# Attention and feed-forward kernel: queries made up to three slots ahead, projection first in a slot, transpose back behind the division

## The reference

```python
def _layernorm(x): return (x - mean(x)) / sqrt(var(x) + eps)      # over the last axis
x = x + attention(_layernorm(x), ctx, ctx, mask)                  # 16 heads of 16, scores: exp(log_C) * tanh(q.k * scale / 4)
x = x + ffn(_layernorm(x))
def ffn(x):
    gf = sigmoid-net of x.mean(axis=1)                            # 3 layers, per batch
    out = x
    for _ in range(3):
        tf = sigmoid-net of out                                   # 4 layers, per token
        coupling = 0.1 + adaptive_range * (0.7*gf + 0.3*tf - 0.5) * 2.0
        out = out + coupling * twist(out)                         # [p_r, -p_i, -o_r, o_i]
    return out
```

## Time and profile before

| | |
|---|---|
| median of 3 runs | 1152.38 us (1148.89 to 1153.36) |
| profiled execution | 1158.11 us, span 1156.2 us |
| mean granted TensorE clock | 0.964 |
| TensorE matmul busy | 998.3 us (86%) |
| ScalarE busy | 928.4 us (80%) |
| VectorE busy | 793.2 us (69%) |
| GpSimd busy | 584.0 us (51%) |
| 16 DMA engines, mean | 13.0% |

### The profile page before, as it was taken

How to read it: one execution, slowest core, us unless ns; L and a number is a source line. 1 busy time by engine, 2 the same in 40 slices (tenths; PEclk the granted TensorE clock), 3 DMA queues, 4 the chain that set the end, 5 groups by cost and what they waited for, 6 DMA issues and landing times.

```text
span 1156.2 us, 21972 instructions
## 1 busy us (share of the span) xinstructions
PE 998.3 (86%) x7260; PEld 536.9 (46%) x7260; DVE 793.2 (69%) x1738; ACT 928.4 (80%) x1153; POOL 584.0 (51%) x1117
## 2 busy tenths in 40 slices
PE   6889988899888998889888898888988889886894
PEld 4555435544455434554355543555435544453431
DVE  4876677757687485874858749577577757676285
ACT  5999679887798777987779877898679887794576
POOL 4577107871188602895048830688207871175303
PEclk8999999999999998999999999999999999997897
DMA  4110002210022100211002200122001220010002
GB/s 129 45 42 19 1 2 68 65 50 1 1 69 69 46 1 2 89 48 46 1 24 69 69 23 2 45 70 69 0 1 47 69 68 1 1 42 28 19 1 74
DMA packets 67281, 43.85 MB, mean 38 GB/s; under 512 B 42081, under 2 KB 50785, under 8 KB 67169
## 3 DMA queue, kind: packets, MB, share of 16 engines
q1 hardware_dynamic: 67168, 42.45, 13.0%
HBM read 25.51 MB, written 16.78 MB: 37 GB/s over the span
## 4 chain that ended last, share of the span: by engine, by line
PE 41%; DVE 21%; issue 14%; ACT 12%; POOL 10%; SPq 1%; DVEq 0%; DMA 0%; POOLq 0%; ACTq 0%
PE ps L1098 7%; PE ps L1143 7%; PE ps L1130 7%; PE ps L1156 5%; ACT probs L835 5%; PE ps L1067 4%; DVE move_u L727 4%; PE ps L1083 3%; ACT probs L841 3%; DVE coup L693 2%; DVE f_t L731 2%; PE ps L1186 2%; DVE move_u L706 2%; DVE move_v L708 2%; PE ps L1165 2%
## 5 line engine op out<-in xcount | busy, mean ns | idle before, releaser
L835 ACT ACTIVATE probs<-ps,u_scale 120x2048 f32<-120x2048 f32 x128 | 253.4, 1980 | 41.5 <-PE ps L1067 40.7
L841 ACT ACTIVATE probs<-probs,exp_bias,clip 120x2048 f32<-120x2048 f32 x128 | 269.5, 2106 | 0.1
L1156 PE MATMUL ps<-h,w 128*128 128x512 f32 x384 | 184.2, 605 | 14.0 <-ACT h L867 13.2
L1067 PE MATMUL ps<-q_t,k_t 32*120 32x256 f32 x2048 | 154.0, 416 | 32.0 <-ACT probs L835 31.2
L447 POOL TENSOR_TENSOR c<-tok_c 128x16 f32<-128x16 f32 x8 | 1.8, 222 | 330.7 <-issue 330.7
L637 DVE STREAM_TRANSPOSE o_t<-ps 128x512 f32<-128x512 f32 x128 | 91.2, 712 | 99.7 <-PE ps L1083 99.6
L1098 PE MATMUL ps<-wo_t,of_t 128*128 128x256 f32 x512 | 149.1, 417 | 8.5 <-DVE of_t L657 8.5
L1083 PE MATMUL ps<-probs,va 120*32 120x256 f32 x2048 | 140.2, 392 | 4.7 <-ACT probs L841 4.7
L1067 PEld LDWEIGHTS ps<-q_t,k_t 32*120 32x120 f32 x2048 | 96.1, 184 | 61.7 <-issue 56.3
L1098 PEld LDWEIGHTS ps<-wo_t,of_t 128*128 128x128 f32 x512 | 94.1, 204 | 44.6 <-issue 26.4
L498 POOL TENSOR_TENSOR f_hl<-f_t,f_hl 128x512 f16<-128x512 f32 x64 | 73.7, 1162 | 79.9 <-DVE f_hl L684 79.9
(11 more groups left out here) (129 smaller groups left out, 1849.6 us busy)
## 6 DMA issues: line engine op xcount, KB each, us to landing
xy<-in_x_dram SPq DMA_DIRECT2D x64, 256.0 KB, 2.9
out_dram<-xy SPq DMA_DIRECT2D x64, 256.0 KB, 2.0
cbuf<-in_ctx_dram SPq DMA_DIRECT2D x64, 120.0 KB, 2.7
tok_c<-coup SPq DMA_DIRECT2D x256, 0.5 KB, 2.0
move_v<-in_L_xattn_W_out_dram SPq DMA_DIRECT2D x1, 256.0 KB, 5.3
move_u<-in_L_ffn_cn_w_dram SPq DMA_DIRECT2D x1, 256.0 KB, 5.6
w<-in_L_ffn_cn_w_dram SPq DMA_DIRECT2D x1, 128.0 KB, 5.5
g<-in_L_ffn_gc_w_dram SPq DMA_DIRECT2D x1, 128.0 KB, 4.0
```

The costliest lines, as they stand in the source:

```text
L835: eng.activation(probs[:, b % 2, n * HALF:(n + 1) * HALF, :].rearrange("k h q -> k (h q)"), banks(SCORE_BANK, 4)[0:KEYS, :], ACT.Tanh, sca ...
L841: eng.activation(p, p, ACT.Exp, scale=clip[0:KEYS, 0:1], bias=exp_bias[:, b:b + 1]).then_inc(s_exp, 1)
L1067: last = eng.matmul(banks(SCORE_BANK + r)[0:KEYS, odd * S:(odd + 1) * S], k_t[rows, b % 2, odd, n, :], q_t[rows, b % 2, n, :], start=True, ...
L1156: last = eng.matmul(banks(bank), w2[:, k, :], h1[:, p % 2, k, :], start=(k == 0), stop=(k == EK - 1))
```

## The change

- q_hat and its statistics get four buffers (QR). Three queries a group instead of one are made in the feed-forward stage (early+2 to early+4, two before high half 2, one before high half 3); the slots at 0, 1 and 4 make none, the slots at 2 and 3 make that of i+3, the others that of i+2. Slots before 11 go on making i+2.
- GpSimd's query_hat is split into query_scale and query_hat, norm_2 into norm_2_scale and norm_2, factors into twisted_part and x_part, and they are put in another order within a slot.
- VectorE runs residual(i-2) and stats_2(i-2) first in a slot, and attn_features(i-1) directly behind divide(i-1), one slot earlier than before. The high halves move from the slots at 3 and 5 to those at 2 and 4.
- TensorE runs project(i-2,0) and project(i-2,1) directly behind scores(i,0). keys(i+1) stays behind scores(i,1), weighted_values(i-1,1) follows it.
- SyncE loads before it stores, and the load of i+4 that fell into the slot at 0 is issued in the feed-forward stage.

```diff
+    QR = 4
...
-        mv1 = sb("mv1", [P, 2, TT, 2])
+        mv1 = sb("mv1", [P, QR, TT, 2])
...
-        q_hat = sb("q_hat", [P, 2, TT, E])
+        q_hat = sb("q_hat", [P, QR, TT, E])
...
-        HIGH_AT = (3, 5)
+        HIGH_AT = (2, 4)
...
+        def ahead_in_slot(i):
+
+            if i < GROUP + LAG:
+                return i + 2 if i >= 0 else None
+            at = (i - LAG) % GROUP
+            return None if at in (0, 1, 4) else i + 3 if at < 4 else i + 2
+
+        def ahead_in_ffn(g):
+
+            early = g * GROUP + GROUP + LAG
+            return [b for b in range(early + 2, early + 5) if b < NB]
...
                 if kind != "attention":
+                    for b in ahead_in_ffn(i)[2:]:
+                        load(b)
                     coupling_rows(i)
...
-                for b in late[:1]:
-                    store(b)
-                late = late[1:]
...
-                elif 0 <= i + 4 < NB and i >= -1:
+                elif 0 <= i + 4 < NB and i >= -1 and not after_ffn(i):
                     load(i + 4)
+                for b in late[:1]:
+                    store(b)
+                late = late[1:]
...
                 if kind == "ffn":
-                    early = i * GROUP + GROUP + LAG
-                    if early + 2 < NB:
-                        query_hat(early + 2)
-                    for chunk in (2, 3):
-                        for k in range(EK):
-                            low_half(i, chunk, k)
+                    ahead = ahead_in_ffn(i)
+                    for b in ahead[:2]:
+                        query_scale(b)
+                        query_hat(b)
+                    for k in range(EK):
+                        low_half(i, 2, k)
+                    for b in ahead[2:]:
+                        query_scale(b)
+                        query_hat(b)
+                    for k in range(EK):
+                        low_half(i, 3, k)
...
                 if 0 <= i - LAG < NB:
+                    norm_2_scale(i - LAG)
+                    if after_ffn(i):
+                        norm_2(i - LAG)
+                        coefficients(groups_before(i) - 1)
+                for b in late[:1]:
+                    twisted_part(b)
+                if 0 <= i - LAG < NB and not after_ffn(i):
                     norm_2(i - LAG)
-                if i == early:
-                    coefficients((i - LAG) // GROUP - 1)
+                if new is not None and 2 <= new < NB:
+                    query_scale(new)
                 for b in late[:1]:
-                    factors(b)
+                    x_part(b)
                 late = late[1:]
                 if 0 <= i + 1 < NB:
                     values(i + 1)
...
+                if new is not None and 2 <= new < NB:
+                    query_hat(new)
...
-                    new, nxt, here, old = i + 2, i + 1, i - 1, i - 2
+                    new, nxt, here, old = ahead_in_slot(i), i + 1, i - 1, i - 2
...
+                    if 0 <= old < NB:
+                        residual(old)
+                        stats_2(old)
                     if 0 <= here < NB:
                         attn_out(here, 0)
-                    if 0 <= old < NB:
-                        attn_features(old)
                     if 0 <= nxt < NB:
                         queries_out(nxt)
                         keys_out(nxt)
-                    if 2 <= new < NB and i != early:
+                    if new is not None and 2 <= new < NB:
                         stats(new)
                     if 0 <= here < NB:
                         attn_out(here, 1)
-                    if 0 <= old < NB:
-                        residual(old)
-                    if 0 <= here < NB:
                         divide(here)
-                    if 0 <= old < NB:
-                        stats_2(old)
+                        attn_features(here)
                     for b in late[:1]:
                         combine(b)
...
-                    early = i * GROUP + GROUP + LAG
-                    if early + 2 < NB:
-                        stats(early + 2)
+                    ahead = ahead_in_ffn(i)
+                    for b in ahead[:2]:
+                        stats(b)
                     high_half(i, 2)
+                    for b in ahead[2:]:
+                        stats(b)
                     high_half(i, 3)
...
                     if 0 <= i < NB and i != early:
                         scores(i, 0)
+                    if 0 <= old < NB:
+                        project(old, 0)
+                        project(old, 1)
                     if 0 <= here < NB:
                         weighted_values(here, 0)
...
                     if 0 <= nxt < NB:
                         keys(nxt)
-                    if 0 <= old < NB:
-                        project(old, 0)
                     if 0 <= here < NB:
                         weighted_values(here, 1)
-                    if 0 <= old < NB:
-                        project(old, 1)
                     if 0 <= i - LAG < NB:
                         norm_to_features(i - LAG)
```

More of the change, by code:

```diff
@@ L422, in norm_2 @@
                 eng.tensor_tensor(rstd2[:, at, :], var2[:, b % 2, :], minus_half[:], ALU.pow).then_inc(s_rstd2, 1)
+            def norm_2(b):
+                at = b % XR
                 eng.wait_ge(s_neg2, b + 1)
@@ L499, in low_half @@
                    .then_inc(s_flo, 1)
-            early, late = None, []
+            late = []
             for kind, i in slots():
                 if kind == "ffn":
-                    early = i * GROUP + GROUP + LAG
-                    if early + 2 < NB:
-                        query_hat(early + 2)
-                    for chunk in (2, 3):
-                        for k in range(EK):
-                            low_half(i, chunk, k)
+                    ahead = ahead_in_ffn(i)
[9 more added lines that the diff above has]
+                        low_half(i, 3, k)
                     late = list(range(i * GROUP, (i + 1) * GROUP))
                     continue
-                if 0 <= i - LAG < NB:
+                new = ahead_in_slot(i)
+                if i == -2:
+                    for b in range(2):
+                        query_scale(b)
+                        query_hat(b)
+                if 0 <= i - LAG < NB:
+                    norm_2_scale(i - LAG)
[5 more added lines that the diff above has]
+                if 0 <= i - LAG < NB and not after_ffn(i):
                     norm_2(i - LAG)
-                if i == early:
-                    coefficients((i - LAG) // GROUP - 1)
+                if new is not None and 2 <= new < NB:
+                    query_scale(new)
                 for b in late[:1]:
-                    factors(b)
+                    x_part(b)
                 late = late[1:]
@@ L757, in end_combine @@
                    .then_inc(s_res, 1)
-            late, early = [], None
+            late = []
             for kind, i in slots():
```

47 lines of the change are left out of this document (23 added, 24 removed).

## The result

| | before | after |
|---|---|---|
| median | 1152.79 us (4 runs, 1148.89 to 1153.36) | 1168.71 us (4 runs, 1167.17 to 1170.21) |
| profiled execution | 1158.11 us, span 1156.2 us | 1167.66 us, span 1165.9 us |
| mean granted TensorE clock | 0.964 | 0.986 |

The changed kernel is slower: the ratio is 1.0145, 95% interval 1.0118 to 1.0173. The forecast was 1220 us with a range of 1178 to 1260, so the side was right and the size was far off.

A forecast was written before the change was run, and what follows sets the result against it. ScalarE's 8.39 us of work was taken to bound a slot, with 35 us lost to late q_hat. From the 1152.4 us median, +32 without the clock and +37 for it (+69) gave 1220 us, range 1178 to 1260.

The forecast's parts named there:

- The ring: Attention slots: residual(i-2), all of VectorE's slot, project(i-1) on TensorE, residual(i-1) form a closed chain of 10.0 us against 8.39.
- Its length: The closed chain's step times in an attention slot, summed: 10.0 us with new stats, 9.5 us without.
- a step that needs the result just made is its duration + 0.10: Rule for dependent VectorE steps, start to start: 0.10 us added to the duration, as reciprocal 0.35, next 0.45 later.
- the sum without the clock: Whole kernel before any clock loss: slots 2 to 10 +14.4, groups +23, feed-forward starts -2, last group +3.5, drain -7; +32.
- The clock: TensorE idling before projections lowers its clock: 1.0 us per slot with stats, 0.25 without, +37 us.
- If it falls in the middle of the projection, about 1.4 us of that runs at half speed: TensorE's projection after 1.9 us idling: low clock adds 1.4 us a slot, bounds 0 and 1.9, taken as 1.0 with stats.
- the first rival: TensorE's idle pieces come out shorter or spread, so the slot chain costs without clock loss: 1184 us, chance 0.2.
- The second rival: Low TensorE clock in nearly every attention slot, 54 x 1.4 = 76 us more: 1260 us, chance 0.15.
- My 10 of 12: TensorE's idle pieces of 1.84 to 2.36 us in the late groups before: the clock fell to 0.50 after 10 of 12.
- The waits for q_hat: TensorE's waits before query transposes in later groups go, regaining 5.9 us a group, 35 us in six groups.
- Edits costed at nothing: Extra feed-forward stats and q_hat, SyncE's moved load, high halves at slots 2 and 4: each priced 0.
- The drain: Last tanh to first feed-forward matmul, 28.9 us, becomes some 22 with the transpose back right behind the division: -7 us.

The follow-up runs named there:

- the kernel with the longer ring: Changed kernel plus one more 128x512 transpose into a spare tile on VectorE, in front of the second output transpose: 1220.00 us, ratio 1.0578.
- the one with the residual behind: Changed kernel with VectorE's residual(i-2) and stats_2(i-2) moved from the slot's start to behind the transpose back: 1198.50 us, ratio 1.0402.
- the first experiment: Changed kernel with VectorE's and TensorE's slot orders put back; queries ahead and GpSimd's new order stay: 1168.83 us, ratio 1.0123 against the kernel before.
- the fastest kernel: Kernel before plus queries ahead, high halves between query and key copy, GpSimd's low half in front of the factors: 1138.59 us, ratio 0.9861.
- the kernel with early high halves: Kernel before plus queries ahead, old slot orders, high halves at slots 2 and 4 instead of 3 and 5: 1151.29 us, ratio 0.9960.

## Why the prediction was right or wrong

**The ring: right.** It was built from rows of the kernel before, and every link stands in the timeline of after in the order foretold. The order alone makes it, a longer VectorE slot makes it longer by just that, and without the order the first group is at 8.39 us again.

**Its length: 10.0 forecast, 9.63 measured.** The step that failed here is "a step that needs the result just made is its duration + 0.10". That was read off the reciprocal, and it holds for it (0.46 from its start to the division's, duration 0.35). Behind the larger instructions the extra is 0.03 to 0.04: residual to stats_2 0.73 (forecast 0.79), second output transpose to reciprocal 0.73 (0.81), division to transpose back 0.72 (0.79), 0.21 of the 0.37 us. The rest lies behind: the transpose back overlaps nothing, 0.71 + 0.06 to the projection (0.67 + 0.15), then 2.03 to the residual (2.13). Without stats the residuals are 9.3 to 9.5 us apart (forecast 9.5). In a group, four intervals with stats and three without gave 66.6 us for 68.5. The first residual of a group comes 1.66 us behind the first tanh instead of 2.1. These two make the groups' 13.6 of the 22 us by which the sum without the clock was too high. The rest is the drain (2.8), the feed-forward stages (2.3 and 0.8), the first group (1.7) and the last (1.0).

**The clock: wrong, and the largest error.** The step "If it falls in the middle of the projection, about 1.4 us of that runs at half speed", taken at 1.0 per slot with stats (and 0.25 without), was +37 us of the +69. It was worth 0, and what came is the first rival, the ring without the clock, in a shorter ring. The idle piece in front of the projection is there, 1.51 to 1.52 us in the slots with stats (forecast 1.9), and the granted clock doesn't fall to 0.50 anywhere between 34 and 1082 us of the changed kernel, with 25 idle pieces of 1.3 to 1.6 us, 21 of 1.0 to 1.3 and three of 1.6 to 2.5 in front of projections. The 10 falls of the kernel before behind its waits for q_hat are gone as well. The price was misread too: those falls came 0.9 us behind the restart on average and not half a us, which leaves 1.2 us of a projection of 2.1 to slow down and not 1.4. The second rival's rule came from the Trainium skill ("TensorE: Matmul & The Clock Gate", section on HAM oscillation): a recurring wait can bring the low clock on every round. The page's case is a wait for a DMA that is longer than any wait in front of a projection in the changed kernel, so it did not bear out what the rival made of it, a low clock in all 54 slots. This trace has a wait in every slot of the ring, and the clock held. I was half right that length matters: the idle was 1.5 us and not 1.9, since the ring is shorter. But length isn't all. In the kernel with the longer ring, TensorE's timeline and the windows show both outcomes:

```profile
240.97 2.54 PE L1141 MATMUL ps<-wo_t,of_t 128*128 128x256 f32 x8 [2.43 <-DVE of_t L701]
...
252.32 3.63 PE L1141 MATMUL ps<-wo_t,of_t 128*128 128x256 f32 x8 [1.81 <-DVE of_t L701]
```

```profile
243.00:244.00 1.00, 1.00 (x10) 0.33 (x12) 0.45 (x1) 0.65 (x1) 1.00 (x3) 0.50 0.17 55
```

Behind 1.81 us of idling most of a projection ran at the 1.2 GHz level (3.63 us for 1.99); behind 2.02 to 2.12 us in every slot of the first group it never did. In front of projections in attention slots, 11 of 49 idle pieces of 1.6 to 3.0 us were followed by the low clock in that kernel, and 8 of 34 in the one with the residual behind. Elsewhere it nearly always was: 5 of 6 in front of the query transposes in the kernel with queries ahead alone (1.84 to 1.97 us), and 10 of 12 in front of the key transposes in that of the first experiment (only 1.61 to 1.64 us). My 10 of 12 was read among the old order's instructions and applied to the new one's, which the rows didn't cover. What makes the difference is open.

**The waits for q_hat: right that they go, wrong in what they are worth.** There are none over 1 us in the changed kernel. But the kernel with queries ahead alone, which has the old orders, gained 11 us in the groups and not 35: six of these waits stayed, and the slots at 4 and 6 stayed at 9.2 us. In the changed kernel the ring hides nearly all that is left of the gain: with the order alone TensorE has no such wait of over 1 us either, and the queries ahead are worth 0.7 us a group. That the groups lose only 1.6 us each, while a slot of the ring is 1.24 longer than ScalarE's, is because their slots took 9.2 us on average before and not 8.39.

**Edits costed at nothing.** The high halves at slots 2 and 4 hold no combine in the changed kernel, by the new orders of VectorE and TensorE; with the old ones they cost 9 us. No run has the changed kernel with them at 3 and 5, so that they cost 0 there isn't shown. GpSimd's new order had no term in the sum at all: with the old orders of VectorE and TensorE it cost 17 us, in the changed kernel its price isn't known. VectorE now waits up to 2.2 us for the load of x in front of the stats (13.0 us in seven waits), yet the stats and loads in the feed-forward stages cost nothing: these stages became shorter.

**The drain: right in kind.** -9.8 us for -7. The transpose back right behind the division, by itself, took 3.1 us off it (27.4 to 24.3, on the kernel with queries ahead); with all of the order and the queries as before it is 19.9. So most of it needs the projection and the residual first in the slot as well.

## What to carry to other kernels

When an order is changed, follow the result of the first instruction of an engine's slot until it comes back to the same engine; if that way holds the whole slot, its length is the new pace, and what is moved off it pays until the next longest way sets the pace (0.45 us a slot of a call of 0.88). Before such a call is moved, list who waits for it: each of the three calls moved off this ring was on another way (a PSUM bank, GpSimd's statistics, or none that was longer, which was the one that paid). A change of many parts hides a good one: here the queries ahead gained 1.1% alone, and an order that gains only in the drain and the starts of the feed-forward stages took it back.

## What the runs showed of the hardware

- VectorE's combine (128x256 float32, two tensors read from SBUF) takes 0.42 us, and up to 1.38 us while GpSimd subtracts one tensor from another; with one tensor read by GpSimd 0.87 at most. The division, 0.69 us, took 1.42 beside a GpSimd instruction that reads one tensor. It goes the other way too: in the changed kernel GpSimd's x part (two instructions) started at 780.51 us, 0.19 us behind the division, and took 1.47 us, where it took 1.10 in the fastest kernel. The Trainium skill ("SBUF — State Buffer", on the shared port pair) says that of a VectorE instruction with two inputs in SBUF and a GpSimd instruction that reads SBUF, the one that starts first has the pair for the whole instruction and the other blocks. The subtraction fits that (the held combine ended 0.28 us behind it), the division roughly (it ended 0.91 us behind the x part, and takes 0.69 alone). The combine of 0.83 us that began and ended within GpSimd's one-input instruction of 1.70 us doesn't.
- A microsecond on VectorE can cost two on TensorE: behind a combine held by 0.96 us TensorE idled 1.40 us and ran at the low clock, and in the kernel with early high halves four of the twelve slots at 4 and 6 took 11.1 to 11.2 us instead of the 9.2 of the kernel with the late ones.
- The granted clock isn't a function of the length of the idle piece alone, as told above: 2.02 to 2.12 us in every slot of one group left it at 1.00, 1.81 us elsewhere did not.
